# A setup that sends two loads first, takes its shift from one product, norms its squarings by an earlier matrix and shares one program with the first layer

## The chip, the cores and the metric

The kernel runs on one core of a Trainium2 chip. The metric is the device time of one execution in microseconds. The median of three runs of the kernel before is 2298.62 us (2295.13 to 2299.04). The trace comes from one profiled execution of it.

## The reference

The input x has 128 graphs of 64 nodes with 256 features, and there is one adjacency matrix `adj` of 64 x 64. Four layers follow each other, each as `x = layernorm(x + layer(x, ...))`: a graph transformer block, a graph convolution with LSTM windows, a graph convolution with batch norms, and an attention over neighbours. The change touches what is made from `adj` before layer 0, and the part that needs the most work there is the largest eigenvalue in layer 0:

```python
eig = jnp.linalg.eigvalsh(L)            # L is adj here
lam_max = eig[-1] + 1e-08
L_norm = 2.0 * L / lam_max - jnp.eye(N, dtype=L.dtype)
xp = jnp.einsum('mn,bnf->bmf', L_norm, x)
h = xp @ Wc + bc
...
```

The later layers use other tables made from `adj`: its symmetric normalisation with the degrees (layer 2), masks (layers 0 and 3), and a matrix that mixes a parent with its children (layer 3).

## The kernel before

The kernel gets the largest eigenvalue by repeated squaring. With S = (adj + adj transposed) / 2 it finds the largest row sum s of absolute values, forms P = (S + s I) / s, and squares P 24 times; the dominating eigenvector is then all that is left, and a Rayleigh quotient gives the eigenvalue. In every fourth squaring the result is divided by the sum of squares of the matrix that is squared. The squarings are in a loop on TensorE (L620 to L628) and on VectorE (L572 to L588): TensorE squares into PSUM (L624), VectorE copies the result back to SBUF (L585). In the fourth of a round VectorE multiplies P with itself and sums each row (L577, L579), TensorE adds the rows up with a product with ones (L627), VectorE takes the reciprocal (L581) and scales the square on its way to SBUF (L587).

Around this chain stand the other parts of the setup. SyncE sends 39 loads in order: six small loads of `adj` and its transpose into block-diagonal 128 x 128 tiles (L455 to L457, after two memsets), ten small tables (L460 to L463), the weights of layer 0 (L465), nine rows of its vectors (L468), the first x of the four streams (L470), and weights of layer 1 (L472, L473). GpSimd makes the degrees' and mask tables (L496 to L526). The float32 weights of four products are split into a high and a low part: ScalarE copies them into the high part (L536), GpSimd subtracts (L530). The end of the chain is `lnormT` (L601, L602), and behind it VectorE writes three late tables, `refineT`, `ahatT` and `bg0_rows` (L604 to L609).

The setup is a block of its own: it ends with `end_phase()` (L448 onward in the trace, the semaphores are cleared and all engines meet in a barrier, L143), and layer 0 is the next block. Layer 0 works on groups of 256 tokens in four streams and eight turns. The order of the steps on each engine is written out by `weave` from a table of ticks (`plan0`), which lets stream 3 run ahead: its mix with lnormT (slot 0, L291) is the first product of layer 0, and the streams 2, 1 and 0 follow. TensorE's slot 0 waits for the stream's x (`xs_loaded`) and for `var2_ready`, which VectorE hands out at the beginning of its part of layer 0 by `ahead`. The first step of GpSimd in layer 0 is the layer norm of stream 3 (L356). Every wait is a semaphore; nothing waits for a time.

In the listings `arena` and `H` are the names of SBUF regions in which many tiles lie, `ps` is PSUM. `alone` is an increment of a semaphore that nobody waits for, which keeps a wait apart from the product behind it.

## Time and profile before

| what | value |
|---|---|
| median of three runs | 2298.62 us |
| lowest and highest run | 2295.13, 2299.04 us |
| profiled execution, span from the first to the last instruction | 2298.5 us |
| TensorE busy | 2138.9 us, 93% |
| VectorE busy | 1384.4 us, 60% |
| ScalarE busy | 1153.9 us, 50% |
| GpSimd busy | 440.6 us, 19% |
| mean granted TensorE clock | 0.979 |

The profiled execution has no time of its own apart from its span, which lies 0.1 us from the median of the runs. The busy share is a mean over the whole program; the setup is its first 43 us, and there the timeline has to be read, in which each row is one instruction, or several of one kind, with its start and length.

### The profile page before, as it was taken

The numbers are of one execution on the slowest core, as the hardware profiler recorded it, in microseconds if no ns is written. First come the engines' busy times: TensorE is split into PE (matmuls) and PEld (weight loads), VectorE is DVE, ScalarE is ACT, GpSimd is POOL, SyncE is SP. The second block draws the span as 40 slices with busy tenths as digits, with TensorE's granted clock in tenths as the row PEclk, the third lists the DMA queues.
The fourth block names the chain that finished last, engine by engine and source line by source line (L and its number), as shares of the span: only waits on it lengthen the run. The fifth ranks groups of instructions, "written<-read, shape, count | busy, mean of one in ns | idle before, by whom it ended". The sixth has DMA issues, their size and how long they took to land. (4 is left out here: it accounts for less than half of the span.)

```text
span 2298.5 us, 44203 instructions
## 1 busy us (share of the span) xinstructions
PE 2138.9 (93%) x17360; PEld 1878.8 (82%) x17360; DVE 1384.4 (60%) x2703; ACT 1153.9 (50%) x2183; POOL 440.6 (19%) x876
## 2 busy tenths in 40 slices
PE   4999999999969989999999999999999797979998
PEld 3888888888869978888888889988888786858886
DVE  4788788878866644443344434354443677956776
ACT  1444454355433357644444534443533565648886
POOL 3344344434430000000000000000000221014554
PEclk9999999999999999999999999999999899989999
DMA  3110111011013201000000000000000331001221
GB/s 99 34 56 19 41 50 55 9 46 55 28 40 109 63 30 37 1 19 1 1 1 19 19 1 1 1 1 1 1 1 1 114 119 60 1 28 60 79 76 51
DMA packets 76401, 81.86 MB, mean 36 GB/s; under 512 B 6544, under 2 KB 74000, under 8 KB 75408
## 3 DMA queue, kind: packets, MB, share of 16 engines
q1 hardware_dynamic: 76304, 80.51, 11.1%
q8 instruction: 67, 1.10, 0.2%
q14 instruction: 30, 0.25, 0.0%
HBM read 55.33 MB, written 25.17 MB: 35 GB/s over the span
## 5 line engine op out<-in xcount | busy, mean ns | idle before, releaser
L323 PE MATMUL ps<-R 128*128 128x256 f32 (+3 forms) x8136 | 1494.5, 344 | 38.5 <-DVE R L1545 12.9
L323 PEld LDWEIGHTS ps<-R 128*128 128x128 f32 x8136 | 1313.5, 191 | 202.1 <-DVE R L802 15.7
L1226 ACT ACTIVATE late_half<-ps,lstm_bias 128x512 f32<-128x512 f32 (+2 forms) x460 | 283.4, 669 | 382.1 <-PE ps L323 382.0
L365 POOL TENSOR_TENSOR ln_veps<-ln_mv,eps_tile 128x2 f32<-128x2 f32 x128 | 28.6, 223 | 1313.9 <-DVE ln_mv L348 1313.9
L864 PE MATMUL ps<-H 128*128 128x256 f32 x1024 | 238.3, 382 | 3.1 <-ACT H L785 1.7
L864 PEld LDWEIGHTS ps<-H 128*128 128x128 f32 x1024 | 188.9, 191 | 26.5 <-ACT H L785 1.9
L1261 DVE TENSOR_TENSOR late_half<-late_half 128x1024 f32<-128x1024 f32 (+2 forms) x32 | 37.6, 1176 | 186.4 <-ACT late_half L1226 186.4
L1223 ACT ACTIVATE late_half<-late_half 128x1024 f32<-128x1024 f32 (+2 forms) x66 | 68.1, 1032 | 124.4 <-DVE late_half L1266 78.4
L1263 DVE TENSOR_TENSOR late_half<-late_half 128x1024 f32<-128x1024 f32 (+2 forms) x32 | 37.6, 1176 | 132.6 <-ACT late_half L1226 132.6
L391 DVE SCALAR_TENSOR_TENSOR H<-H,ln_rstd 128x256 f32<-128x256 f32 x192 | 106.5, 595 | 6.8 <-POOL ln_rstd L358 3.3
L1270 DVE TENSOR_TENSOR H<-late_half 128x1024 f32<-128x1024 f32 (+2 forms) x34 | 45.9, 1349 | 89.9 <-ACT late_half L1226 89.9
L344 DVE BATCH_NORM_STATS2 ln_stats<-H 128x6 f32<-128x256 f32 x256 | 96.0, 417 | 5.3 <-POOL H L746 2.0
L1245 DVE TENSOR_TENSOR R<-H,R 128x1024 fp32r<-128x1024 f32 (+2 forms) x66 | 95.7, 1451 | 1.3 <-ACT R L1206 1.1
L1206 ACT ACTIVATE R<-H 128x1024 fp32r<-128x1024 f32 (+2 forms) x66 | 94.6, 1434 | 0.0
L368 POOL TENSOR_TENSOR ln_rstd<-ln_veps,minus_half 128x2 f32<-128x2 f32 x128 | 90.0, 703 | 10.0
L386 DVE SCALAR_TENSOR_TENSOR H<-H,ln_mv 128x256 f32<-128x256 f32 x192 | 90.6, 512 | 2.2 <-issue 1.6
L1273 DVE TENSOR_TENSOR late_half<-late_half 128x1024 f32<-128x1024 f32 (+2 forms) x32 | 37.7, 1177 | 81.2 <-ACT late_half L1226 81.2
L785 ACT ACTIVATE H<-ps,b_col 128x256 f32<-128x256 f32 x128 | 50.3, 476 | 68.4 <-PE ps L323 68.4
L348 DVE BATCH_NORM_AGGREGATE ln_mv<-ln_stats 128x2 f32<-128x6 f32 x448 | 55.7, 166 | 33.7 <-DVE ln_stats L344 19.7
L376 ACT ACTIVATE H_state<-H_state,ln_shift,ln_rstd 128x256 f32<-128x256 f32 x128 | 69.9, 602 | 11.4 <-POOL ln_shift L370 11.4
L1259 DVE TENSOR_TENSOR late_half<-late_half 128x1024 f32<-128x1024 f32 (+2 forms) x34 | 40.9, 1201 | 57.6 <-ACT late_half L1226 57.6
L356 POOL TENSOR_TENSOR ln_veps<-ln_mv,eps_tile 128x2 f32<-128x2 f32 x96 | 21.7, 226 | 269.0 <-DVE ln_mv L348 269.0
(211 smaller groups left out, 2668.7 us busy)
## 6 DMA issues: line engine op xcount, KB each, us to landing
H<-in_x SPq DMA_DIRECT2D x64, 256.0 KB, 4.1
residual<-H SPq DMA_DIRECT2D x32, 256.0 KB, 2.2
H<-residual SPq DMA_DIRECT2D x32, 256.0 KB, 4.0
arena<-residual SPq DMA_DIRECT2D x32, 256.0 KB, 2.8
residual<-arena SPq DMA_DIRECT2D x32, 256.0 KB, 2.2
H_state<-residual SPq DMA_DIRECT2D x32, 256.0 KB, 2.7
out<-H_state SPq DMA_DIRECT2D x32, 256.0 KB, 2.2
arena<-in_wih SPq DMA_DIRECT2D x4, 1024.0 KB, 4.8
```

The costliest lines, as they stand in the source:

```text
L323: mm = pe.matmul(out, lhsT(a), rhs(b), start=start and n == 0, stop=stop and n == len(PASSES) - 1)
L344: c.step(dve.bn_stats(ln_stats[:, s, n, :], y[:, n, :]))
L348: ins = dve.bn_aggr(ln_mv[:, s, n, :], ln_stats[:, s, n, :])
L368: c.step(pool.tensor_tensor(ln_rstd[:, s, :], ln_veps[:, s, :], minus_half[:, 0:TILES], ALU.pow))
L376: ins = act.activation(y[:, n, :], y[:, n, :], ACT.Identity, bias=ln_shift[:, s, n:n + 1], scale=ln_rstd[:, s, n:n + 1])
L386: c.step(dve.scalar_tensor_tensor(out=y[:, n, :], in0=y[:, n, :], scalar=ln_mv[:, s, n, 0:1], in1=g, op0=ALU.subtract, op1=ALU.mult))
L391: ins = dve.scalar_tensor_tensor(out=y[:, n, :], in0=y[:, n, :], scalar=ln_rstd[:, s, n:n + 1], in1=be, op0=ALU.mult, op1=ALU.add)
L864: mm = pe.matmul(out[:, n, :], src[:, k, n * P:(n + 1) * P], w[:, k, :], start=(k == 0), stop=(k == blocks - 1))
L1206: act.activation(x.as_window(xin[x.s][:, 0]), x.window(), ACT.Copy).then_inc(x_hi[x.s], 1)
L1223: act.activation(x.part(bg), x.part(cell[s]), ACT.Tanh).then_inc(tanh_ready[s], 1)
L1226: ins = act.activation(into[q][:, m, 0:x.cols], gate_ps(q, m, x.cols), ACT.Tanh if q == TANH_G else ACT.Sigmoid, bias=lstm_bias[:, x.p - 1 ...
L1245: dve.tensor_tensor(x.as_window(xin[x.s][:, 1]), x.window(), x.as_window(raw(xin[x.s][:, 0])), ALU.subtract).then_inc(x_ready[x.s], 1)
```

## The change

The constant `RUN` goes from 4 to 3, and the setup's block is gone: what each engine did there now stands at the beginning of its part of layer 0, without the clearing and the barrier in between. Within that:

- SyncE sends `adj` and its transpose first, into tiles of their own, with no wait (`s_loaded`). Then it waits for the memsets and sends five more. Alpha, gamma and the x of stream 0 come before the weights; the other three x and the eight small tables come after the weights and rows.
- S is no longer halved, and the shift is the maximum over one product: ones times the absolute values of S, with one more column that holds 1e-30. P is S times the reciprocal plus the identity, in one instruction. The halves reappear in the last constants (4.0 and 0.5e-8).
- The squarings are written out, without a loop. In each run of three the norm comes from the first matrix: its multiply and sum while it is squared, its trace product behind the second squaring, and the third square is scaled twice by a factor that stands for that norm. The row sums for the degrees are spread over the second squarings of runs 2, 3 and 4 (`sums`).
- TensorE does the last product with S and the trace product before the products for the late tables, which now lie in bank 7 of PSUM. lnormT is one instruction.
- GpSimd makes mask0 and `ident_r` early, then the degree tables and `refine`, then the splits, and only then the bias tables of layer 3.
- In layer 0, TensorE waits once for the weights, the tables and lnormT, and in its first slot 0 of stream 3 for `late_made`, which VectorE sends behind the late tables.

The core of the diff (names and declarations left out; the removed setup is in the listing above):

```diff
-RUN = 4
+RUN = 3
...
         @block.sync
         def _(sp):
+            sp.dma_start(adj2[0:NODES], t["adj"]).then_inc(s_loaded, 16)
+            sp.dma_start(turned_adj[0:NODES], t["adjT"]).then_inc(s_loaded, 16)
+            sp.wait_ge(zeroed, 2)
+            for g in range(2):
+                r = slice(NODES * g, NODES * (g + 1))
+                sp.dma_start(adjT[r, r], t["adjT"]).then_inc(adj_loaded, 16)
+                sp.dma_start(adj_bd[r, r], t["adj"]).then_inc(adj_loaded, 16)
+            sp.dma_start(adj2[NODES:P], t["adj"]).then_inc(adj_loaded, 16)
+            sp.dma_start(scal[:, 0:1], rows("alpha")).then_inc(scal_loaded, 16)
+            sp.dma_start(scal[:, 1:2], rows("gamma")).then_inc(scal_loaded, 16)
+            sp.dma_start(tiles_of(xs[0]), rows_of_group(x_rows, 0, 0)).then_inc(xs_loaded[0], 16)
+            for dst, name in ((Wc, "Wc"), (Wq, "Wq"), (Wk, "Wk"), (Wv, "Wv"), (Wo, "Wo"), (W1, "W1"), (W2, "W2")):
...
+            for s in range(1, STREAMS):
+                sp.dma_start(tiles_of(xs[s]), rows_of_group(x_rows, s, 0)).then_inc(xs_loaded[s], 16)
+            for dst, name in ((lstm_b2[:, 0], "lstm_bih"), (lstm_b2[:, 1], "lstm_bhh"), (b1_col[:], "b1"),
+                              (bn1_col[:], "bn1"), (bn2_col[:], "bn2"), (qk3_bias[:], "qk3b"), (col[:, 8:10], "bg0")):
+                sp.dma_start(dst, t[name]).then_inc(small_loaded, 16)
+            sp.dma_start(bv3_col[:], t["bv3"]).then_inc(small_loaded, 16)
...
         @block.gpsimd
         def _(pool):
+            pool.memset(absS, 1e-30).then_inc(pool_made, 1)
+            pool.memset(ones, 1.0).then_inc(pool_made, 1)
+            pool.memset(ident[:], 0.0).then_inc(pool_made, 1)
+            pool.memset(adjT[:], 0.0).then_inc(zeroed, 1)
+            pool.memset(adj_bd, 0.0).then_inc(zeroed, 1)
...
+            pool.wait_ge(adj_loaded, 80)
+            pool.wait_ge(pool_made, 7)
+
...
+            for n, (split, w) in enumerate(splits0):
+                pool.wait_ge(w0_hi, n + 1)
+                pool.tensor_tensor(split[:, 1], w, raw(split[:, 0]), ALU.subtract).then_inc(w0_split, 1)
+
+            link(pool.tensor_scalar(masked, adj_bd, 0.0, -NEG, ALU.is_equal, ALU.mult))
+            link(pool.tensor_tensor(far, far, masked, ALU.add))
...
+            pool.wait_ge(small_loaded, 8 * 16)
+            link(pool.tensor_scalar(qk3_bias[:, 0:1], qk3_bias[:, 0:1], float(ATT3) ** -0.5, None, ALU.mult))
+            link(pool.tensor_tensor(lstm_bias[:], lstm_b2[:, 0], lstm_b2[:, 1], ALU.add))
+            pool.wait_ge(w0_loaded, 16 * 16)
...
         @block.scalar
         def _(act):
+            act.wait_ge(w0_loaded, 16 * 16)
+            for split, w in splits0:
+                act.activation(split[:, 0], w, ACT.Copy).then_inc(w0_hi, 1)
+            act.wait_ge(small_loaded, 8 * 16)
```

VectorE and TensorE:

```diff
+            def sums(part):
+
+                if part == 1:
+                    dve.wait_ge(sums_asked, 1)
...
+            dve.wait_ge(s_loaded, 32)
+            link(dve.tensor_tensor(S64[0:NODES], adj2[0:NODES], turned_adj[0:NODES], ALU.add))
+            dve.wait_ge(pool_made, 2)
+            dve.scalar_tensor_tensor(out=absS[0:NODES, 0:NODES], in0=S64[0:NODES], scalar=-1.0, in1=S64[0:NODES],
+                                     op0=ALU.mult, op1=ALU.max).then_inc(sq_ready, 1)
+            dve.wait_ge(small_mm, 1)
+            link(dve.tensor_reduce(col[0:NODES, 10:11], ps0(1)[0:NODES, 0:NODES + 1], AX_X, ALU.max))
+            link(dve.reciprocal(col[0:NODES, 11:12], col[0:NODES, 10:11]))
+            dve.wait_ge(pool_made, 4)
+            dve.scalar_tensor_tensor(out=P64[0:NODES], in0=S64[0:NODES], scalar=col[0:NODES, 11:12],
+                                     in1=ident[0:NODES, 0:NODES], op0=ALU.mult, op1=ALU.add).then_inc(p_ready, 1)
+
+            for n in range(SQUARINGS):
+                if n % RUN == 0:
+                    dve.wait_ge(p_ready, n + 1)
+                    link(dve.tensor_tensor(M64[0:NODES], P64[0:NODES], P64[0:NODES], ALU.mult))
+                    dve.tensor_reduce(col[0:NODES, 12:13], M64[0:NODES], AX_X, ALU.add).then_inc(q_ready, 1)
+                if n % RUN == 1:
+                    sums(n // RUN)
+                if n % RUN == 2:
+                    dve.wait_ge(tr_ready, n // RUN + 1)
+                    link(dve.reciprocal(col[0:NODES, 13:14], ps0(4)[0:NODES, 0:1]))
+                    link(dve.tensor_scalar(col[0:NODES, 14:15], col[0:NODES, 13:14], float(NODES),
+                                           col[0:NODES, 13:14], ALU.mult, ALU.mult))
+                dve.wait_ge(squared, n + 1)
+                if n % RUN == RUN - 1:
+                    dve.tensor_scalar(P64[0:NODES], ps0(3)[0:NODES, 0:NODES], col[0:NODES, 14:15],
+                                      col[0:NODES, 14:15], ALU.mult, ALU.mult).then_inc(p_ready, 1)
+                else:
+                    dve.tensor_copy(P64[0:NODES], ps0(3)[0:NODES, 0:NODES]).then_inc(p_ready, 1)
+
+            dve.wait_ge(p_ready, SQUARINGS + 1)
+            link(dve.scalar_tensor_tensor(out=M64[0:NODES], in0=P64[0:NODES], scalar=4.0, in1=P64[0:NODES],
+                                          op0=ALU.mult, op1=ALU.mult))
+            link(dve.tensor_reduce(col[0:NODES, 15:16], M64[0:NODES], AX_X, ALU.add))
+            dve.wait_ge(small_mm, 2)
+            link(dve.tensor_tensor(M64[0:NODES], P64[0:NODES], ps0(3)[0:NODES, 0:NODES], ALU.mult))
+            dve.tensor_reduce(col[0:NODES, 14:15], M64[0:NODES], AX_X, ALU.add).then_inc(sq_ready, 1)
+            dve.wait_ge(small_mm, 3)
+            dve.wait_ge(adj_loaded, 80)
+            link(dve.reciprocal(col[:, 12:13], ps0(2)[:, 1:2]))
+            link(dve.tensor_scalar(col[:, 13:14], ps0(2)[:, 0:1], col[:, 12:13], 0.5e-8, ALU.mult, ALU.add))
+            link(dve.reciprocal(col[:, 12:13], col[:, 13:14]))
+            dve.scalar_tensor_tensor(out=lnormT[:], in0=adjT[:], scalar=col[:, 12:13], in1=ident[:],
+                                     op0=ALU.mult, op1=ALU.subtract).then_inc(lnorm_ready, 1)
+            dve.wait_ge(spread_done, 1)
+            dve.wait_ge(small_loaded, 8 * 16)
+            link(dve.tensor_copy(refineT[:], refine_ps))
+            link(dve.tensor_tensor(ahatT[:], abdT, spread[:, 0:P], ALU.mult))
+            for k in range(KD):
+                link(dve.tensor_scalar(bg0_rows[:, k, :], spread[:, P:P + NODES], col[:, 8 + k:9 + k], None,
+                                       ALU.mult))
+            dve.sem_inc(late_made, 1)
+            dve.wait_ge(w0_loaded, 16 * 16)
+
             steps = Steps(dve, "l0_dve", {1: 1 + LN_STATS, 2: LN_AFFINE, 8: 2, 11: 1 + LN_STATS,
...
         @block.tensor
         def _(pe):
+            pe.wait_ge(sq_ready, 1)
+            pe.wait_ge(pool_made, 2)
+            pe.matmul(ps0(1)[0:NODES, 0:NODES + 1], ones[0:NODES, 0:NODES], absS[0:NODES],
+                      start=True, stop=True).then_inc(small_mm, 1)
+            for n in range(SQUARINGS):
+                pe.wait_ge(p_ready, n + 1)
+                pe.matmul(ps0(3)[0:NODES, 0:NODES], P64[0:NODES], P64[0:NODES], start=True, stop=True)\
+                  .then_inc(squared, 1)
+                if n % RUN == 1:
+                    pe.wait_ge(q_ready, n // RUN + 1)
+                    pe.matmul(ps0(4)[:, 0:1], ones[0:NODES, :], col[0:NODES, 12:13],
+                              start=True, stop=True).then_inc(tr_ready, 1)
+            pe.wait_ge(p_ready, SQUARINGS + 1)
+            pe.matmul(ps0(3)[0:NODES, 0:NODES], S64[0:NODES], P64[0:NODES], start=True, stop=True)\
+              .then_inc(small_mm, 1)
+            pe.wait_ge(sq_ready, 2)
+            pe.matmul(ps0(2)[:, 0:2], ones[0:NODES, :], col[0:NODES, 14:16], start=True, stop=True)\
+              .then_inc(small_mm, 1)
+            pe.wait_ge(spread_asked, 1)
+            pe.wait_ge(pool_made, 7)
+            pe.matmul(spread[:, 0:P], ones, ddinv, start=True, stop=True)
+            pe.matmul(spread[:, P:2 * P], ones, big, start=True, stop=True)
+            pe.wait_ge(refine_made, 1)
+            pe.transpose(refine_ps, refine, ident[:]).then_inc(spread_done, 1)
+            pe.wait_ge(w0_loaded, 16 * 16)
+            pe.wait_ge(tables_made, 1)
+            pe.wait_ge(lnorm_ready, 1)
+
             def product(out, src, w, blocks=KD):
 
...
             def stage(s, slot, turn):
                 if slot == 0:
+                    if first(turn) and s == STREAMS - 1:
+                        pe.wait_ge(late_made, 1)
```

SyncE at the beginning of the program, before. The names are destination and source:

```order
L455 DMA adjT<-in_adjT 64x64 [waits zeroed]
L456 DMA arena<-in_adj 64x64
L457 DMA arena<-in_adj 64x64
L455 DMA adjT<-in_adjT 64x64
L456 DMA arena<-in_adj 64x64
L457 DMA arena<-in_adj 64x64
L460 DMA arena<-in_lstm_bih 128x32
```

The same place after; `s_loaded` is signalled by the first two rows:

```order
L514 DMA arena<-in_adj 64x64
L515 DMA arena<-in_adjT 64x64
L519 DMA adjT<-in_adjT 64x64 [waits zeroed]
L520 DMA arena<-in_adj 64x64
L519 DMA adjT<-in_adjT 64x64
L520 DMA arena<-in_adj 64x64
L521 DMA arena<-in_adj 64x64
L522 DMA scal<-in_alpha 128x1
L523 DMA scal<-in_gamma 128x1
L524 DMA H<-in_x 128x2x256
L526 DMA H<-in_Wc 128x512
```

The loads of `adj` that the eigenvalue needs stand in front of the wait, and the weights' first load moved from the 17th place to the 11th. The small tables, in rows 7 and on of before, now follow the last x.

VectorE in one round of squarings, before (from the third copy of a round to the scaled one; REGISTER_ALU and ISA belong to the loop's waits):

```order
L585 COPY arena<-ps 64x64 [waits squared]
L576 REGISTER_ALU
L577 TENSOR_TENSOR arena<-arena 64x64 [waits p_ready]
L86 ISA
L579 TENSOR_REDUCE arena<-arena 64x1 [waits sq_steps]
L580 REGISTER_ALU
L581 RECIPROCAL arena<-ps 64x1 [waits tr_ready]
L86 REGISTER_ALU
L587 TENSOR_SCALAR arena<-ps,arena 64x64 [waits squared,sq_steps]
```

VectorE in the first run of three after:

```order
L737 TENSOR_TENSOR arena<-arena 64x64 [waits p_ready]
L738 TENSOR_REDUCE arena<-arena 64x1 [waits small_steps]
L751 COPY arena<-ps 64x64 [waits squared] x2
L743 RECIPROCAL arena<-ps 64x1 [waits tr_ready]
L744 TENSOR_SCALAR arena<-arena 64x1 [waits small_steps]
L748 TENSOR_SCALAR arena<-ps,arena 64x64 [waits squared,small_steps]
```

The multiply and the sum stand in front of the run's first copy now, and the reciprocal, with one more small scaling, in front of its last.

TensorE at the end of the setup, before:

```order
L630 MATMUL ps<-arena 128x128 [waits spread_asked]
L631 MATMUL ps<-arena 128x128
L633 MATMUL ps<-ident,arena 128x128 [waits refine_made]
L635 MATMUL ps<-arena 64x64 [waits p_ready]
L638 MATMUL ps<-arena 128x2 [waits sq_ready]
L448 UNCONDITIONAL_BRANCH
L858 UNCONDITIONAL_BRANCH [waits barrier_Pool_Activation_PE_DVE_SP_release]
L291 MATMUL ps<-lnormT,H 64x64 [waits xs_loaded3,var2_ready3]
```

TensorE at the same place after:

```order
L849 MATMUL ps<-arena 64x64 [waits p_ready]
L856 MATMUL ps<-arena 64x64 [waits p_ready]
L859 MATMUL ps<-arena 128x2 [waits sq_ready]
L863 MATMUL ps<-arena 128x128 [waits pool_made,spread_asked]
L864 MATMUL ps<-arena 128x128
L866 MATMUL ps<-ident,arena 128x128 [waits refine_made]
L291 MATMUL ps<-lnormT,H 64x64 [waits xs_loaded3,late_made,var2_ready3,lnorm_ready,w0_loaded,tables_made]
L291 MATMUL ps<-lnormT,H 64x64 x15
```

The last product with S and the trace product moved in front of the three for the late tables, two block changes are gone, and the first product of layer 0 carries four more waits.

## Rows read from the trace of the kernel before

**Rows 1.** The page: its first line, and TensorE's busy share by slice.

```profile
span 2298.5 us, 44203 instructions
...
PE   4999999999969989999999999999999797979998
```

**Rows 2.** SyncE's waits (total, times, longest); timeline of loads and shift (start, length, us).

```profile
SPq L455 <- POOL arena L478: 0.4, 1, 0.4
...
4.28 0.60 SPq L457 DMA_DIRECT2D arena<-in_adj  x1
...
6.29 0.22 DVE L548 TENSOR_TENSOR arena<-arena,adjT 64x64 f32<-64x64 f32 x1 [6.29 <-DMA arena<-in_adj]
...
9.12 0.25 DVE L562 TENSOR_SCALAR arena<-arena 64x64 f32<-64x64 f32 x1
```

**Rows 3.** Timeline, VectorE and TensorE in one round of four squarings.

```profile
18.55 0.28 DVE L587 TENSOR_SCALAR arena<-ps,arena 64x64 f32<-64x64 f32 x1
...
18.94 0.28 PEld L624 LDWEIGHTS ps<-arena 64*64 64x64 f32 x2 [0.71 <-issue]
...
19.45 0.22 DVE L585 COPY arena<-ps 64x64 f32<-64x64 f32 x1 [0.62 <-PE ps L624]
...
21.39 0.22 DVE L577 TENSOR_TENSOR arena<-arena 64x64 f32<-64x64 f32 x1
...
21.47 0.28 PEld L624 LDWEIGHTS ps<-arena 64*64 64x64 f32 x2 [0.56 <-issue]
...
21.64 0.21 DVE L579 TENSOR_REDUCE arena<-arena 64x1 f32<-64x64 f32 x1
...
21.91 0.50 PEld L627 LDWEIGHTS ps<-arena 64*128 64x128 f32 x2 [0.15 <-DVE arena L579]
...
22.53 0.16 DVE L581 RECIPROCAL arena<-ps 64x1 f32<-64x1 f32 x1 [0.68 <-PE ps L627]
...
22.73 0.28 DVE L587 TENSOR_SCALAR arena<-ps,arena 64x64 f32<-64x64 f32 x1
```

**Rows 4.** Timeline of the weights' split; its longest subtraction (groups by shape: busy, mean ns).

```profile
26.38 2.61 ACT L536 ACTIVATE R<-H 128x512 fp32r<-128x512 f32 x4 [24.37 <-DMA H<-in_be]
...
27.16 6.01 POOL L530 TENSOR_TENSOR R<-H,R 128x512 fp32r<-128x512 f32 x4 [4.82 <-ACT R L536]
...
29.73 1.22 DVE L577 TENSOR_TENSOR arena<-arena 64x64 f32<-64x64 f32 x1
...
L530 POOL TENSOR_TENSOR R<-H,R 128x1024 fp32r<-128x1024 f32 x1 | 2.3, 2330 | 0.0
```

**Rows 5.** Timeline, from the last squaring to layer 0's first product.

```profile
35.93 0.80 PE L630 MATMUL ps<-arena 128*128 128x128 f32 x2
...
36.23 0.28 DVE L587 TENSOR_SCALAR arena<-ps,arena 64x64 f32<-64x64 f32 x1
...
37.29 0.29 PEld L635 LDWEIGHTS ps<-arena 64*64 64x64 f32 x2 [0.33 <-issue]
...
39.98 0.29 DVE L602 TENSOR_TENSOR lnormT<-lnormT,ident 128x128 f32<-128x128 f32 x1
...
40.96 0.60 DVE L609 TENSOR_SCALAR bg_rows<-ps,arena 128x64 f32<-128x64 f32 x2
...
43.00 1.13 PE L291 MATMUL ps<-lnormT,H 64*64 64x64 f32 x32 [4.03 <-DVEq L63]
```

**Rows 6.** Timeline of SyncE's queue: the first weight, the four loads of x.

```profile
9.81 0.43 SPq L465 DMA_DIRECT2D H<-in_Wc  x1
...
17.61 5.32 SPq L470 DMA_DIRECT2D H<-in_x  x4
```

**Rows 7.** GpSimd: first work in layer 0 (timeline); longest table operation (groups by shape).

```profile
50.42 0.20 POOL L356 TENSOR_TENSOR ln_veps<-ln_mv,eps_tile 128x2 f32<-128x2 f32 x1 [17.25 <-DVE ln_mv L348]
...
L513 POOL TENSOR_SCALAR arena<-arena 128x128 f32<-128x128 f32 x1 | 0.7, 657 | 0.1
```

**Rows 8.** Window of 55 to 58.5 us: busy us of each engine, then the granted clock.

```profile
55.00:58.50 3.50, 3.18 (x15) 3.18 (x16) 3.02 (x9) 0.20 (x1) 1.30 (x3) 0.52 0.12 42
```

More of the change, by code:

```diff
@@ L421, in build_program @@
     col = sq(16)
-    S64, P64, M64, eye_s = (sq(NODES) for _ in range(4))
+    S64, P64, M64, turned_adj = (sq(NODES) for _ in range(4))
+    absS = sq(NODES + 1)
     abd, abdT, diag, ddinv = sq(P), sq(P), sq(P), sq(P)
@@ L429, in ps0 @@
         return ps[:, b, :]
+    spread = ps0(7)[:, 0:2 * P]
+    refine_ps = ps0(7)[:, 2 * P:3 * P]
     zeroed = psem("zeroed")
@@ L434, in build_program @@
     pool_made = psem("pool_made")
+    s_loaded = psem("s_loaded")
     adj_loaded = psem("adj_loaded")
+    scal_loaded = psem("scal_loaded")
     deg_ready = psem("deg_ready")
@@ L641, in build_program, with first @@
-    end_phase()
+    refine_made = psem("refine_made")
+    tables_made, lnorm_ready, late_made = psem("tables_made"), psem("lnorm_ready"), psem("late_made")
+    def first(turn):
+        return isinstance(turn, int) and turn == 0
     xr0, zt_words, hbuf, x1, vt, x1b, x2b = ([buf(G2) for _ in S] for _ in range(7))
@@ new lines, in _ @@
+            link(pool.tensor_tensor(abdT, adjT[:], ident[:], ALU.add))
+            link(pool.tensor_tensor(diag, abd, ident[:], ALU.mult))
+            pool.sem_inc(sums_asked, 1)
+            pool.wait_ge(scal_loaded, 32)
+            for g in range(2):
+                r, other = (slice(NODES * h, NODES * (h + 1)) for h in (g, 1 - g))
+                link(pool.memset(far[r, r], 0.0))
+                link(pool.memset(far[r, other], -OTHER_GRAPH))
+            link(pool.tensor_scalar(mask0[:], adj2, 0.0, -NEG, ALU.is_le, ALU.mult))
@@ L793, in _, with link @@
         def _(dve):
+            small = Chain(dve, small_steps)
+            def link(ins):
+                small.step(ins)
+                small.settle()
+            def sums(part):
+                if part == 1:
+                    dve.wait_ge(sums_asked, 1)
+                    link(dve.tensor_reduce(col[:, 1:2], abd, AX_X, ALU.add))
+                    link(dve.tensor_reduce(col[:, 2:3], abdT, AX_X, ALU.add))
+                if part == 2:
+                    link(dve.tensor_reduce(col[:, 3:4], diag, AX_X, ALU.add))
+                    link(dve.tensor_reduce(col[:, 0:1], adj2, AX_X, ALU.add))
+                if part == 3:
+                    link(dve.tensor_tensor(col[:, 4:5], col[:, 1:2], col[:, 2:3], ALU.add))
+                    dve.tensor_tensor(col[:, 4:5], col[:, 4:5], col[:, 3:4], ALU.subtract).then_inc(deg_ready, 1)
@@ L904, in stage @@
                 if slot == 4:
+                    if first(turn) and s == 0:
+                        pe.wait_ge(w0_split, len(splits0))
                     pe.wait_ge(fm_ready[s], FM * turn + 1)
```

212 lines of the change are left out of this document (36 added, 176 removed).

## The prediction

> **What bounds the kernel now.** I read the page first, then the timeline of the first 70 us, then the waits of SyncE's queue and the groups by shape for durations. The page shows a span of 2298.5 us and TensorE busy for over 90% of nearly every slice except the first, where it has four tenths [rows 1]. So the program is a chain of TensorE stages, and the change touches only its head: everything before layer 0's first product, which starts at 43.00 [rows 5]. That head is a chain of tiny dependent steps. VectorE cannot start until the sixth load has landed (issued 4.28, landed 6.29), and the shifted matrix is ready at 9.37 [rows 2]. In a round of four squarings a plain one costs 0.84 us: the matrix is ready at 18.83, TensorE starts 0.11 later, VectorE copies from 19.45 to 19.67. The fourth costs 1.66, since the norm's multiply, sum, product and reciprocal come one after the other; a round is 23.01 - 18.83 = 4.18 [rows 3]. The last matrix is ready at 36.51, lnormT at 40.27, the late tables at 41.56, and the program's end with its barrier takes the 1.44 us to 43.00 [rows 5]. After that layer 0 runs from semaphores alone, in the same order in both kernels, so I carry a shift of that first product through to the end one for one. The sum is made against the profiled span, 2298.5; the three runs have 2295.1 to 2299.0 with a median of 2298.6, so the two agree, and the runs differ among themselves by 3.9.
>
> **The change part by part.** Times below are from the span's start.
>
> Loads. SyncE now waits 0.4 us for two memsets, then issues a load each 0.64 (0.60 and a small gap), the sixth at 4.28 [rows 2]; so it could have started at about 0.68. The two loads now sent first leave at 0.68 and 1.32, and with the 2.01 us that the sixth took they are there at 3.35, not 6.29: 2.9 saved.
>
> Shift. Before, 6.29 to 9.37 is 3.08 [rows 2]. Now it is an addition 0.25, an absolute value 0.28, one product with its evacuation 0.62, a maximum 0.24, a reciprocal 0.20 and a fused multiply-add 0.28, with a gap of 0.03 each, the durations of their likes in the squarings [rows 3]. That is 1.87: ready at 5.2, another 1.2 saved.
>
> Squarings. Three to a run, eight runs. The multiply and the sum (21.39 to 21.85) lie inside the 0.62 in which TensorE squares [rows 3]. The trace product goes behind the second squaring: from the second matrix, 0.11 + 0.44 until TensorE takes it, 0.62 to its result, 0.38 for a reciprocal and the new small scaling, so the factor is there at 1.55. The third squaring is held by the trace product's weight load (0.50) to 1.05 and done at 1.56, scaled at 1.85. A run is 0.84 + 1.85 = 2.69, eight are 21.5; before it was 9.37 to 36.51, 27.1. So the last matrix stands at 26.7 instead of 36.51. Below this, the sequencer's extra increment in front of each squaring goes (0.11 with it, 0.06 for the trace product without it [rows 3]), up to 24 x 0.05 = 1.2 more. The row sums, two short reductions in each of two squarings, are hidden behind the 0.62 if GpSimd's three additions are done by then. They need the last of five loads, issued at 4.5 and landed at 6.5; they wait at the fifth squaring, near 8.7, and only 0.7 us or so of slack covers them.
>
> End of the setup. Before, 36.51 to 40.27 is 3.76; TensorE now does the last product at once, not behind the three for the later tables (35.93 to 37.29, which held it 0.67), and lnormT takes one instruction of 0.3 less. That leaves 2.8: lnormT at 29.5. The three products come next and end near 29.8. The late tables still cost 1.29, and TensorE waits for them: the first stream to start is stream 3, which waits for late_made, and VectorE hands out var2_ready only behind them. So they are not hidden. The barrier (1.44) becomes five increments and a wait, between 0.11 and 1.44; at 0.05 an increment I take 0.3. Without any collision layer 0 starts at 31.4, 11.6 us earlier.
>
> The collision. The weights land at 26.38 and are split by GpSimd from 27.16 to 33.17, the last split alone 2.33 long [rows 4]. SyncE reaches the first weight after seven loads of 0.64, two of 0.45 and one x of 1.33 (a quarter of 5.32 [rows 6]), at 7.4 instead of 9.81, so I move the landing to 24.0 and the splits to 24.8 to 30.8. In before, only one norm multiply fell into the splits, and it took 1.22 instead of 0.22 [rows 4]: VectorE reads two operands there, as it does in the multiply of 26.7 and in the one for lnormT. Cost: nothing if these forms do not collide, at most the rest of one split each. By the nearest row I take it: lnormT waits until 30.8, is done at 31.1, and layer 0 starts at 31.1 + 1.29 + 0.3 = 32.7 at the latest, 32.5 as my value because the chain may get in before the long split.
>
> On such collisions the Trainium skill (SBUF — State Buffer, "SBUF: two separate sides") says that VectorE and GpSimd share one pair of ports under an exclusive lock: a VectorE operation with two SBUF inputs waits for the whole GpSimd operation if that one started first. The stretched multiply agrees in size; no run here yet shows the fused form that makes lnormT. By the rule the start is 32.7, without it 31.4.
>
> What is covered. The other tables go behind the splits on GpSimd: eight operations of at most 0.66 [rows 7], so GpSimd is free by 36.1. Layer 0 first needs it 7.4 us after its start (50.42 against 43.00), at 40. The small loads now leave last, the eighth near 23, behind weights and x; I expect them at 27, since three x and eight small loads stand between them and the weights' 24.0. Three engines wait for them: behind VectorE's wait stand the late tables and with them TensorE's start, behind GpSimd's the first step of layer 0, behind ScalarE's its first copy there. Before 29.8 none of these is due. x of stream 3 leaves after the weights and lands ahead of the start too.
>
> Sum: 43.0 - 32.5 = 10.5 us; 2298.5 - 10.5 = **2288.0 us**, own range 2285.5 to 2290.5.
>
> **Rivals.**
> - No collision, and the increments count. The start is 30.2 to 31.4, the time 2285.7 to 2286.9. For it: the splits collide with one multiply in six only. Against it: no other multiply lay in their way.
> - The loads become the bound. The small ones land late: all weights, rows and x are in the queue in front of them. If the small loads land at 33, the late tables end at 34.3 and layer 0 starts at 34.6, 8.4 earlier: 2290; at 36 it is 2293. For it: in before the weights, issued from 9.81 on, had landed only at 26.38 [rows 4, 6], so the queue is deep. Against it: everything in that queue leaves 2.4 us earlier.
> - The head was not the bound: layer 0's static order absorbs the shift, and the time stays at 2298. For it: only that GpSimd and the loads keep their own times. Against it: GpSimd has 4 us of slack, and no engine waits for an absolute time.
> - Slower: the clock. From 55 to 58.5, early in layer 0, the granted clock is 0.52 on average, that is mostly the lower level, 1.2 GHz [rows 8]. Moving the start moves where TensorE's short idle times fall, and each further stretch of 3.4 us at the lower level costs at most 1.7 us of TensorE work. From seven further ones (11.9) the 10.5 us are gone; at ten the time is 2288 + 17 = 2305. For it: the clock did fall right after the start. Against it: the order of work, and with it the idle times, is the same as before.
>
> **How the numbers follow.** Forecast 0.60; no collision 0.14; loads 0.14; absorbed 0.07; clock 0.05. A change of up to 0.2%, 4.6 us, cannot be told from none for this kernel. Faster needs less than 2294.0, which the first three cases give: 0.88. Same 0.07, slower 0.05. The range is 2282.5 to 2294.5: below it takes in no collision with a median that falls by the 3 us by which runs differ, above the late loads to 36; the last two cases stay outside.
>
> **What would show it.** VectorE's first addition at 3.4 and the shifted matrix at 5.2 (step one and two); eight runs in 20.5 to 21.5 us with the trace product behind each second squaring; a multiply of over 1 us for lnormT that ends with GpSimd's last split near 30.8; layer 0's first product at 32.5 and its first GpSimd step 7.4 us later. A first product after 38, or a stage of layer 0 that is longer than before by microseconds, would make the prediction wrong.

## The result, and the profile after

The changed kernel takes 2303.84 us (median of 12 runs, 2300.66 to 2310.06) against 2298.4 for the kernel before (12 runs, 2295.13 to 2302.50); the ratio is 1.0025 with a 95% interval of 1.0015 to 1.0036. It is slower by 0.25%, and 15.8 us above the forecast. A run's time is 1.8 us longer than the span of its trace (2302.24 and 2300.4 for the traced execution of the changed kernel); the forecast was worked out from a span.

The setup did what it should. Timeline of the profile after (start, length, us; engine, line, operation), the rows that answer to [rows 2 to 5]:

```profile
3.39 0.22 DVE L723 TENSOR_TENSOR arena<-arena 64x64 f32<-64x64 f32 x1 [3.39 <-DMA arena<-in_adjT]
...
5.18 0.22 DVE L737 TENSOR_TENSOR arena<-arena 64x64 f32<-64x64 f32 x1
...
24.49 2.62 ACT L658 ACTIVATE R<-H 128x512 fp32r<-128x512 f32 x4 [22.48 <-DMA H<-in_be]
...
25.20 6.01 POOL L612 TENSOR_TENSOR R<-H,R 128x512 fp32r<-128x512 f32 x4 [5.67 <-ACT R L658]
...
26.20 0.33 DVE L748 TENSOR_SCALAR arena<-ps,arena 64x64 f32<-64x64 f32 x1
26.57 1.20 DVE L754 SCALAR_TENSOR_TENSOR arena<-arena 64x64 f32<-64x64 f32 x1
...
29.84 1.52 DVE L765 SCALAR_TENSOR_TENSOR lnormT<-adjT,arena,ident 128x128 f32<-128x128 f32 x1
...
31.92 0.60 DVE L772 TENSOR_SCALAR bg_rows<-ps,arena 128x64 f32<-128x64 f32 x2
...
33.22 1.13 PE L291 MATMUL ps<-lnormT,H 64*64 64x64 f32 x32 [2.71 <-DVEq L63]
```

The first addition is at 3.39 (3.35 predicted), the first step on the shifted matrix at 5.18 (5.2), the last matrix stands at 26.20 + 0.33 = 26.53 (26.7), so a run of squarings takes 2.67 (2.69), lnormT's step takes 1.52 and ends at 31.36 with GpSimd's last split (31.1), and layer 0's first product starts at 33.22 where it was 43.00: 9.8 us of the 10.5 are there.

They are gone when layer 1 is under way. Number the ScalarE activations of both traces and take the start of each after less that before; the median of seven neighbours around a time of before is:

| at (us, before) | 60 | 200 | 350 | 430 | 510 | 590 | 690 | 702 | 830 | 2290 |
|---|---|---|---|---|---|---|---|---|---|---|
| after | -10.4 | -10.1 | -10.6 | -8.5 | -7.4 | -5.0 | -5.2 | -0.7 | +1.7 | +1.6 |

Two places take it: layer 0's loop between 350 and 590 (5.6 us), and the start of layer 1's loop at 690 to 702 with what follows to 830 (6.9 us). What is new there stands in TensorE's waits (line waited for and releaser: us in total, times, longest) as waits for nothing that the profile shows:

```profile
PE ps L875 <- issue: 6.1, 3, 2.2
...
PE ps L323 <- issue: 1.5, 1, 1.5
```

The kernel before has neither. L875 is the product that opens a turn of layer 0's loop. A back-branch is the jump from a loop's end to its start; the loop has five. At the third one TensorE stands still:

```profile
350.65 3.08 PE L875 MATMUL ps<-H 128*128 128x256 f32 x8 [1.97 <-issue]
```

The same eight products took 1.89 at 49.22 in this trace; here they run at a granted clock of 0.56 (window 351 to 354). That is no cost beside the kernel before: from 200 to 588 us the mean granted clock is 0.99 in both traces, and behind the second of the three waits it is 1.00 (window 431 to 435). The cause shows in the DMA queues (packets, MB, share of 16 engines). Of before, then of after:

```profile
q8 instruction: 67, 1.10, 0.2%
```

```profile
q8 instruction: 94, 1.54, 0.3%
```

q8 brings TensorE's own program in packets of 16 KB. From 209 to 588 us, four turns of layer 0's loop and most of a fifth, before has no such packet and after has 27. That is nine for each of the three waits: the loop's code is fetched again for a whole turn. Layer 1's loop starts with a wait of its own. TensorE's timeline there, before and after:

```profile
692.01 4.13 PE L291 MATMUL ps<-adjT,H 64*64 64x64 f32 x128 [17.41 <-DMA H<-residual]
696.06 12.02 PE L323 MATMUL ps<-R 128*128 128x256 f32 x96
```

```profile
686.87 3.97 PE L291 MATMUL ps<-adjT,H 64*64 64x64 f32 x128 [17.66 <-DMA H<-residual]
690.77 1.22 PE L323 MATMUL ps<-R 128*128 128x256 f32 x4
693.49 13.70 PE L323 MATMUL ps<-R 128*128 128x256 f32 x90 [1.50 <-issue]
```

Windows of 4 us there (busy us of PE, PEld, DVE, ACT, POOL; then the granted clock, the DMA engines' busy share and GB/s), one of before and three of after:

```profile
694.00:698.00 4.00, 3.89 (x78) 3.61 (x75) 2.59 (x4) 1.79 (x3) 0.00 (x0) 0.67 0.96 374
```

```profile
689.00:693.00 4.00, 2.99 (x64) 2.43 (x57) 2.45 (x4) 1.71 (x3) 0.00 (x0) 0.50 1.00 377
693.00:697.00 4.00, 3.51 (x16) 3.51 (x17) 0.76 (x2) 0.61 (x1) 0.00 (x0) 0.50 0.32 108
697.00:701.00 4.00, 4.00 (x26) 4.00 (x25) 2.07 (x6) 0.65 (x2) 0.00 (x0) 0.68 0.00 0
```

Both traces come to layer 1 at 1.2 GHz (0.50). Before, the clock is back at 2.4 GHz (1.00) some 4.6 us behind the layer's first product: 0.67 is the mean of 2.64 us at 0.50 and 1.36 at 1.00, so it rises at 696.64. After, the wait of 1.5 us comes first, and by the same sum the clock rises at 699.55, 12.7 us behind the first product. Without the wait that is 11.2 us of work at half speed where it was 4.6, so 3.3 us are lost; with the wait it is 4.8, about the 4.5 that the table shows from 690 to 702. Of the 2.4 us that follow up to 830, 1.4 lie in the turns: a turn of layer 1's loop takes 16.31 to 16.40 us here and 16.17 to 16.21 before. What lengthens a turn is open.

### The profile page after: what moved, and what is told of

Read it like the earlier page. It is cut to its first block and busy times, and to the rows that moved or that the text cites. A ratio compares the mean times of both kernels' runs of the same rounds, so it can differ in the third digit from the quotient of the medians.

```text
span 2300.4 us, 44085 instructions
## 1 busy us (share of the span) xinstructions
PE 2144.2 (93%) x17363; PEld 1881.4 (82%) x17363; DVE 1386.2 (60%) x2712; ACT 1153.3 (50%) x2183; POOL 439.8 (19%) x877
## 5 line engine op out<-in xcount | busy, mean ns | idle before, releaser
L323 PE MATMUL ps<-R 128*128 128x256 f32 (+3 forms) x8136 | 1492.4, 344 | 37.1 <-DVE R L1560 13.2
L323 PEld LDWEIGHTS ps<-R 128*128 128x128 f32 x8136 | 1310.9, 190 | 201.3 <-DVE R L1560 13.4
L875 PE MATMUL ps<-H 128*128 128x256 f32 x1024 | 242.5, 387 | 9.3 <-issue 6.1
L875 PEld LDWEIGHTS ps<-H 128*128 128x128 f32 x1024 | 190.9, 193 | 34.1 <-issue 6.7
```

Source lines behind the costliest of these rows:

```text
L323: mm = pe.matmul(out, lhsT(a), rhs(b), start=start and n == 0, stop=stop and n == len(PASSES) - 1)
L875: mm = pe.matmul(out[:, n, :], src[:, k, n * P:(n + 1) * P], w[:, k, :], start=(k == 0), stop=(k == blocks - 1))
```

## The theory and its count

In the compiled program an instruction of TensorE has 64 bytes, so a packet is 256. The trace agrees: in the straight code behind layer 1 a packet comes for every 256 of TensorE's instructions in the median. The squarings, written out instead of a loop of four, put everything behind them 84 instructions later by the compiled program, 94 by the instructions in the traces (see The edge). The body of layer 0's loop is 1632 instructions (104,448 bytes) in both kernels; its back-branch is instruction 3459 before and 3543 after. Theory F: where that body lies decides whether it stays in TensorE's instruction buffer. Rival R: layers 0 and 1 take up any earlier start by their own waits and clock. Rival D: VectorE's loops, 30 instructions later, are what is fetched.

## The first four runs: undo one part, move one program

e1_loop, the changed kernel with TensorE's squarings as a loop again:

```diff
-            for n in range(SQUARINGS):
-                pe.wait_ge(p_ready, n + 1)
+            with pe.Fori(0, SQUARINGS // RUN) as i:
+                for r in range(RUN):
+                    pe.wait_ge(p_ready, RUN * i + r + 1)
+                    alone(pe, waits_passed)
...
```

> The changed kernel with TensorE's 24 squarings as a loop of 8 turns again instead of written out; every other engine as in the changed kernel. TensorE's code ahead of layer 0's loop is then 100 instructions shorter than in the changed kernel and 16 shorter than in the kernel before. Theory F (the changed kernel's later place of TensorE's code makes the back-branches of layer 0's and layer 1's loops wait for instruction fetches, and that costs the 15 us between the 2288.5 that the setup's gain of 9.8 us allows and the 2303.8 measured): no instruction packets between 200 and 580 us, no idle time of 2 us at L875, first product of layer 0 at 33 to 34.5 us, and 2288 to 2291 us. Rival R (the schedule of layer 0 and 1, its clock and its waits take up any earlier start, wherever the code lies): 2302 to 2305. Rival D (it is VectorE's code, 30 instructions later, that has to be fetched again): 2302 to 2305, since VectorE's code is as in the changed kernel.

e2_before_pe84, the kernel before with increments that move TensorE's program alone (g3, j1, j3 and j4 below have another number in the same place; j2 has 100 there in e1_loop's kernel):

```diff
+            for _ in range(84):
+                alone(pe, waits_passed)
             pe.wait_ge(sq_ready, 1)
```

> The kernel before with 84 semaphore increments put at the start of TensorE's program, where it waits for the adjacency's loads; TensorE's loops then begin and end at the same places of its program as in the changed kernel, and the setup stays as before. Theory F: about 8 instruction packets a turn from some 350 us on, idle times of about 2 us at the back-branch of layer 0's loop, a loss by layer 1's loop, and 2298.4 + 15.5 = 2314 us (2308 to 2317). Rivals R and D: 2298.4 (2296 to 2300.5), as the kernel before.

e3_after_pad, the changed kernel with increments in the squarings (g2 below has two each):

```diff
                   .then_inc(squared, 1)
+                for _ in range(7 + (n < 4)):
+                    alone(pe, waits_passed)
```

> The changed kernel with 172 semaphore increments on TensorE, 7 or 8 behind each squaring's product, where it waits for VectorE's copy; its loops then lie 256 instructions (16 KB) further than in the kernel before, so at the same place within a block of 16 KB. Theory F, if the place within a block decides: no refetch in layer 0's loop, 2288 to 2291 us (up to 2 more if the increments delay a squaring). If the place in the whole program decides, not within a block: refetches as in the changed kernel, 2303 to 2306. Rivals R and D: 2303 to 2306.

e4_before_dve30, the same on VectorE:

```diff
+            for _ in range(30):
+                alone(dve, waits_passed)
             dve.wait_ge(adj_loaded, 96)
```

> The kernel before with 30 semaphore increments at the start of VectorE's program, where it waits for the adjacency's loads; VectorE's loops then lie where the changed kernel has them (the back-branch of layer 1's loop at 768 instructions, the end of a block of 16 KB), TensorE's where the kernel before has them. Theory F: as the kernel before, 2298.4 (2296 to 2300.5). Rival D: a loss like the changed kernel's, up to 2314 us. Rival R: 2298.4.

On this chip the kernel before has a median of 2300.68 (26 runs). e1_loop: 2294.22 (9 runs), ratio 0.9971 [0.9959, 0.9982]. Its trace has 67 packets, none of the waits, and the shift goes through to the end:

| at (us, before) | 60 | 200 | 350 | 430 | 510 | 590 | 690 | 702 | 830 | 2290 |
|---|---|---|---|---|---|---|---|---|---|---|
| e1_loop | -9.5 | -9.4 | -9.9 | -9.7 | -9.6 | -9.6 | -9.3 | -9.5 | -9.5 | -9.3 |
| e2_before_pe84 | +6.0 | +6.0 | +6.0 | +6.0 | +6.0 | +6.0 | +6.0 | +9.6 | +11.1 | +10.0 |

Nothing in layers 0 and 1 takes up an earlier start: R falls. The median is 3.2 us above the upper end of the forecast of 2288 to 2291, though the profiled run has 2291.37; the interval reaches from 4 to 9.5 us of gain. e4: 2301.71, ratio 1.0005 [0.9996, 1.0015], 67 packets, no wait: D falls. e2: 2310.28, ratio 1.0038 [1.0025, 1.0051]. Its increments cost 6.0 in the setup, layer 1 loses 3.6 by 702 and 5.1 by 830 after a wait of 1.85, but layer 0 keeps its code, against what F said. The time lies in F's range, 2308 to 2317, by luck: the range counted a loss in layer 0 that did not come and nothing for the increments. e3: 2299.57, not the 2288 to 2291 of F, ratio 0.9992 [0.9980, 1.0004]; 68 packets, neither of the two losses. Its increments cost 6.3 us in the setup (first product 39.55), so a gain of some 4 is left, and its trace loses that again between 1790 and 1900 (see the end). F has the right places but not yet the right rule.

## Four runs on the rule

> The changed kernel once more, unchanged, to see whether what its trace showed comes back. Theory F (instruction fetches of TensorE): 80 to 100 instruction packets of 16 KB on TensorE's queue against 67, waits of about 2 us at the back-branch of layer 0's loop at some or all of its five back-branches, a stall of 1.5 to 1.9 us some 5 us into layer 1's loop with the clock at half for 4 us longer, and about 5 us over the kernel before. Rival N (the refetch in layer 0 was an accident of that one execution): no waits at that back-branch, 67 packets; the stall in layer 1's loop alone, and 2293 to 2297 us.

> The changed kernel with 48 more semaphore increments on TensorE, two behind each squaring's product: by my count from the start of TensorE's program, the body of layer 0's loop then ends 7 instructions into a further block of 256 (16 KB), where the changed kernel's ends 41 ahead of that block and the kernel before's 125 ahead. Theory F, with the block entered that holds the loop's end deciding: refetch in every turn, about 9 packets a turn for four or five turns (100 to 115 in all), a wait of about 2 us at each of the five back-branches, and in layer 0 a loss of 8 to 9 us where the changed kernel's trace had 5.2. Its time: the changed kernel's first product 1.5 us later by the increments, so 2300 to 2308 us with layer 1's stall open. If the blocks don't start where I count them from, or the place isn't what decides: no more packets than the changed kernel has.

> The kernel before with 132 semaphore increments at the start of TensorE's program: layer 0's loop then lies exactly as in the changed kernel with 48 increments more, with the squarings still a loop. The 84 of the run before shifted the setup by 6.0 us, so these shift it by 6.0 + 48 x 0.16 = 13.8. Theory F: refetch in every turn, and a further 8 to 9 us in layer 0 beside what layer 1 loses: 2298.5 + 13.8 + 8.7 = 2321 us (2317 to 2327). If it takes the squarings written out for the refetch to come (rival S): no refetch in layer 0, 2312 to 2316.

g1 (the changed kernel again): 2304.25, before on this chip 2299.9 (29 runs), ratio 1.0017 [1.0004, 1.0030]; 103 packets, four waits at L875, 9.1 us, and 2.4 in layer 1. What the first trace showed comes back. In g2 and g3 the refetch came out as F said: each has 113 packets and a wait at every one of the five back-branches. TensorE's waits of g2 (g3 has 8.9, 5, 2.1):

```profile
PE ps L877 <- issue: 8.8, 5, 1.9
```

Layer 0 lost 7.6 us in g2 (shift -9.2 at 200, -1.6 at 690), and there layer 1 has no wait and loses nothing: 2294.82, ratio 0.9971 [0.9959, 0.9983], 9 us better than the changed kernel with 48 instructions more (3.8 in the spans of the two traces) and below the 2300 to 2308 that were expected with layer 1's stall open. g3: 2320.3 (2321 forecast), partly by luck: 5.3 us are lost in layer 0 where 8 to 9 were expected, and 3.0 between 1790 and 1900 (see the end).

The fourth tried to better e1_loop:

```diff
+            dve.wait_ge(w0_loaded, 16 * 16)
+            ahead(dve, var2_ready, by=2)
             dve.wait_ge(spread_done, 1)
...
-            dve.wait_ge(w0_loaded, 16 * 16)
-            ahead(dve, var2_ready, by=2)
```

> The changed kernel with TensorE's squarings as a loop (as in the first run of this study), and VectorE's first increments that allow layer 0's products handed out ahead of the late tables instead of behind them. In that first run the first product waited for these until 33.67 us, 1.86 after lnormT was there. Theory F and a shift carried one for one: first product at about 31.9, layer 0 without refetch, and 1.5 to 1.9 us under the loop run's (2289 in a trace, 2292.5 in the median). Rival R (the streams' own waits set the pace, stream 3 waits for the late tables as before): the same time as the loop run.

2295.03, no gain, and the first product at 35.09. Stream 3 is the first to start and waits for late_made as well, and this time the multiply of L754 met a longer split and took 2.37 us.

## Layer 1 alone, and a better kernel

i1 moves only layer 1's loop:

```diff
+            for _ in range(48):
+                alone(pe, waits_passed)
             pe.wait_ge(wg_ready, 1)
             with pe.Fori(0, TURNS) as turn:
```

> The changed kernel with 48 semaphore increments on TensorE between layer 0's loop and layer 1's, where TensorE stands idle for 17 us: layer 1's loop alone moves by 48 instructions, to where the run with 48 increments in the squarings had it; setup and layer 0's loop stay as in the changed kernel. Theory F (two separate losses by the place of two loops): layer 0 still refetches at some back-branches (4 to 6 us lost), but no stall at the start of layer 1's loop and its 4.5 to 6.5 us are saved: 2296 to 2300 us. If the loss in layer 1 came from the refetch in layer 0, or from the clock by itself: stall and time as the changed kernel's, 2302 to 2306.

2304.55, ratio 1.0018: the time that I expected did not come. The trace tells why. The wait in L323 is gone, as F has it; but TensorE's idle time ahead of layer 1 became 21.80 where it was 17.66. The increments are not hidden: they run behind the barrier that ends layer 0, one every 0.15 us from 685.42 to 692.77, and layer 1 waits for the last of them:

```profile
693.32 3.69 PE L291 MATMUL ps<-adjT,H 64*64 64x64 f32 x128 [21.80 <-issue]
```

Behind 690 this trace loses 0.8 us to 830, the changed kernel's 6.9. Layer 0 refetched at four back-branches (9.2 us of waits). The time is the one expected if layer 1's stall were no loss of its own; the trace shows another reason, 3.6 us lost ahead of layer 1 by the increments and 8.8 in layer 0.

h1 and h2 go on from g4. h1 puts the late tables' products into a bank of stream 0:

```diff
-    spread = ps0(7)[:, 0:2 * P]
+    spread = ps0(0)[:, 0:2 * P]
...
-                    if first(turn) and s == STREAMS - 1:
+                    if first(turn) and s == 0:
```

> The run with the credits handed out early showed that the first product (stream 3) waits for the late tables, because these are read from stream 3's half of PSUM. Here the tables' products go to a bank of stream 0, and stream 0 waits for them, 11 us later; the rest is that run's kernel. Theory: first product within 0.3 us of lnormT's end, 1.8 us ahead of the loop run's 33.67 unless the exclusive lock of GpSimd's splits holds lnormT longer; shift carried on: 1.5 to 2 us under the loop run. Rival: the streams' waits take it up, the loop run's time.

h2 has that, and GpSimd's splits behind the tables and behind lnormT:

```diff
+            pool.wait_ge(lnorm_ready, 1)
             for n, (split, w) in enumerate(splits0):
```

> The kernel of the run beside it (tables' products in stream 0's bank), and GpSimd's order changed: its six table steps for layer 3's attention ahead of the weights' splits, and the splits behind lnormT, so that none of VectorE's fused steps stands behind a split (in the changed kernel these took 1.20 and 1.52 us, in the kernel before 0.2 to 0.5 for the like). Theory: lnormT some 2 us earlier than in that run, first product at about 30 us, 1.5 to 2 us less in all. Rival: the table steps, now beside the squarings, hold VectorE there for as long as the splits did, no gain.

> The loop run's kernel again, unchanged, on the chip of these runs: 67 packets, no wait at layer 0's back-branch, no stall in layer 1, setup's gain of 9.3 to 9.5 us carried through the layers; 6 to 9.5 us under the kernel before.

Before on this chip: 2300.96 (22 runs). h1: 2291.87, ratio 0.9960 [0.9946, 0.9974]; its first product, 0.2 us behind lnormT, is at 33.65, no sooner than e1_loop's, since a split held L754 for 2.37 us. h2: 2291.08 (2287.45 to 2291.8), ratio 0.9956 [0.9942, 0.9969]; e1_loop again: 2291.69 (11 runs), 0.9969 [0.9958, 0.9980], shift -10.0 at the end. h2's timeline:

```profile
27.47 0.22 DVE L755 SCALAR_TENSOR_TENSOR arena<-arena 64x64 f32<-64x64 f32 x1
...
29.86 0.35 DVE L766 SCALAR_TENSOR_TENSOR lnormT<-adjT,arena,ident 128x128 f32<-128x128 f32 x1
...
30.46 1.13 PE L291 MATMUL ps<-lnormT,H 64*64 64x64 f32 x32
```

Without a split beside them the two fused steps take 0.22 and 0.35 instead of 1.20 and 1.52, the first product is at 30.46, and its shift is -13.0 through both layers; 3.0 of it go between 1790 and 1900, and -9.5 is left at the end. It beats both kernels; its lead over e1_loop is within their intervals.

## The edge

Four more runs, one execution each, on the place at which the changed kernel's loop lies:

> The kernel before with 84 increments once more. Its first trace had no refetch in layer 0, though the loop lies where the changed kernel has it and three traces of such kernels with the squarings written out had refetches at 3, 4 and 4 of the 5 back-branches. If the place is on the edge and chance decides: some refetches here or in the next run. If the written-out squarings are needed at this place: 67 packets again. Layer 1: the stall of 1.5 to 2.4 us at its start again.

> The loop run's kernel with 100 increments at the start of TensorE's program, so that its loops lie exactly where the changed kernel has them, with the setup's order of the changed kernel and the squarings as a loop. Place alone deciding: stall in layer 1, refetches in layer 0 at some back-branches. If the written-out squarings are needed: the stall in layer 1 only.

> The kernel before with 108 increments: the end of layer 0's loop 17 instructions ahead of the place from which the kernel with 132 refetched in every turn (7 behind it), and 24 behind that of the changed kernel. Place alone deciding, with the sequencer reading ahead of the branch: refetch in every turn or nearly, 105 to 113 packets. If the block that the branch itself lies in decides: 67 packets.

> The kernel before with 60 increments: the end of layer 0's loop 24 instructions ahead of the changed kernel's. Place alone deciding: fewer refetches than the changed kernel has or none, 67 to 76 packets; layer 1's loop 24 instructions ahead of where it stalled: stall or not tells how narrow that place is.

They took 2310.23 (j1), 2310.8 (j2), 2321.37 (j3) and 2304.17 us (j4), against 2299.41 for one execution of the kernel before.

The wait at the start of layer 1's loop shows where a block ends. A pass is a weight load and a product, two instructions. In the changed kernel the wait comes behind 132 passes of that loop, in both traces (after and g1): 128 of L291 and 4 of L323, in the rows above. In j2 it comes behind 133 passes, in j3 behind 125, in j4 behind 149, and in e2 and j1 behind 137. In e2:

```profile
702.10 1.55 PE L323 MATMUL ps<-R 128*128 128x256 f32 x9
705.50 10.75 PE L323 MATMUL ps<-R 128*128 128x256 f32 x75 [1.85 <-issue]
```

j3 and j4 lie 24 instructions behind and ahead of e2, and the wait comes 12 passes sooner and later: it stands at one place of the program, and the loop moves under it. So the loops of e2 and j1 do not lie where the changed kernel has them, as the count from the compiled program had said, but 10 instructions ahead, and those of j2 2 ahead. The instructions of TensorE in the traces, up to the first back-branch of layer 0's loop and with one turn of the squarings' loop, say the same: 3494 in the changed kernel, 3484 in e2 and j1, 3492 in j2. Why the compiled program's count is off by 10 is open.

By the count in the compiled program the wait of the changed kernel is 1793 = 7 x 256 + 1 instructions behind the back-branch of layer 0's loop, so that a block begins 1 instruction behind this back-branch if the wait stands at a block's first instruction (the traces' own records give 1785, so the edge itself is certain to some 8 instructions; the order of the kernels is not touched by that). Blocks that begin there cut layer 0's loop like this, with the kernels' places as the traces have them:

| back-branch against the edge, instructions | kernels | blocks under the body | back-branches refetched, of 5 |
|---|---|---|---|
| 102 or 103 ahead | e1 (twice), g4, h1, h2 | 7 | 0 |
| 95 ahead | before, e4 | 7 | 0 |
| 35 ahead | j4 | 7 | 0 |
| 11 ahead | e2, j1 | 7 | 0, 0 |
| 3 ahead | j2 | 7 | 1 |
| 1 ahead | after, g1, i1 | 7 | 3, 4, 4 |
| 13 behind | j3 | 8 | 5 |
| 37 and 47 behind | g3, g2 | 8 | 5, 5 |
| 171 behind | e3 | 7 | 0 |

A body on seven blocks that ends 11 or more instructions ahead of the edge stays; one on eight is fetched again every turn, nine packets each ((113 - 67) / 5 = 9.2; j3 has 112). The changed kernel's loop ends at the edge: some of its back-branches are refetched and some are not, with nine packets a turn as well ((94 - 67) / 3), and what decides from one turn to the next is open. j2, g3 and j3 have the squarings as a loop and refetch, so the written-out form by itself is not needed. Eight blocks with the next one make nine packets, and eight blocks are 128 KB: a buffer of eight that is filled in order, with one block read ahead, fits the rows of 0 and 5; at 3 and 1 instruction ahead it would take a read beyond the branch, which no run tests by itself. The Trainium skill (Runtime: NRT & Kernel Launch, "Instruction fetch mechanics") gives TensorE such a buffer, 128 KiB in blocks of 16 KiB, first in first out, and says that a taken branch to code that is not there stalls until it is fetched. The traces agree, with 1.8 to 2.3 us a time in the mean of a trace, and 3.0 in j2. They don't agree with the two-page window that the same section names: 104 KB loop here without a packet.

Layer 1's wait hangs on the place too: none at 95 to 103 ahead, 0.42 us at 35 ahead, 1.85 and 0.87 at 11, 1.50 at 3, 1.50 and 2.40 at 1 ahead, 3.03 at 13 behind, and none at 37, 47 and 171 behind. In the changed kernel a packet leaves 4.2 us behind the layer's first product, when the layer's loads keep the DMA engines busy (share 1.00 from 689 to 693), and the wait ends 2.4 us later. In g2 and g3 a packet leaves some 24 us ahead of the first product, and there is no wait. That fits a block that is asked for only once the edge before it is passed; no run tests it by itself.

## Why the prediction was wrong

- Loads, shift, squarings, the split's hold on lnormT: right, each within 0.5 us. The rule of the Trainium skill on the exclusive lock (SBUF — State Buffer, "SBUF: two separate sides"), which I had weighed at 31.4 or 32.7, holds for the fused form as well: 1.52 us beside a split in the changed kernel, 0.35 without one in h2. So the rival without a collision did not occur. Nor did that of the late loads: the first late table starts at 31.29, right behind lnormT.
- The 0.7 us between 10.5 and 9.8: the late tables end at 32.52 and the first product is at 33.22. I had 0.3 for what lies between and it is 0.7. lnormT ended 0.26 later than in my sum, with the weights' landing (24.49 for 24.0), and the tables took 1.16 for 1.29. Together that is 0.5 behind the 32.7 of the collision; the other 0.2 I had taken off for a chain that gets in before the long split, and it did not.
- "I carry a shift of that first product through to the end one for one" is the step that failed. The order of work was the same and nothing in it took up the shift: e1_loop, e1b and h2 do carry it through layers 0 and 1, with -9.5, -10.3 and -13.2 at 830. What the step left out is that the program itself has to be delivered. I priced the written-out squarings by the increments that go, and took them to have no other effect. By the place to which they moved two loops they cost 5 to 9 us in layer 0, where the waits for code are 6.1 to 9.2, and 5 to 7 in layer 1, by a wait and the lower clock behind it (after, g1; layer 0 also in i1). No instruction of the setup shows that.
- The rival of the clock had the sign, not the mechanism: in layer 0's loop the mean granted clock is 0.99 as before, and only at layer 1's start does it stay low for longer, with the wait for code; where the code stays (e1_loop), the moved start loses nothing. The absorbed start did not occur at all.
- The range ended at 2294.5, since every case in it was a matter of the first 43 us. The sum also set a span, 2298.5, beside times, which are 1.8 us longer; that is a small part of the 15.8.

## What to carry to other kernels

Written-out code on an engine moves all later code of that engine. Before a change to the length of a program is called free, count the loop bodies behind it in blocks of 16 KB and see on which side of an edge they end. A count from the compiled program was 10 instructions off here, and the edge itself had to be read from the trace. In the profile, a wait for nothing at a loop's first instruction and a higher count on the instruction queue are its marks. Where a gain in one stage is missing at the end, difference the two traces instruction by instruction: the step in that curve is the place.

## What the runs showed that I had not expected

- A semaphore increment on TensorE costs some 0.15 to 0.17 us: in i1 the 48 follow each other every 0.15, and 48 more moved layer 0 by 8.2 us (g3 against e2, +14.2 and +6.0).
- Between 1790 and 1900 us some executions lose up to 4.5 us in steps of 1.5 and others next to nothing (e3, e4, g4 and h1 lose 4.5, h2 and g3 3.0; e1_loop and after next to nothing). From 1790 to 1890 the granted clock is 0.93 in e4, which loses it, and 1.00 in e1_loop, but 0.94 in after, so the clock alone does not tell them apart. It goes with none of the changes. It may be part of the 7 to 10 us by which runs of one kernel differ; its cause is open.
